# Low parts of the attention probabilities: GpSimd works in eight pieces of 416 columns instead of four of 832

## The chip, the core and the metric

The program runs on one core of a Trainium2 chip. A core has five engines that run at the same time and signal each other by semaphores: TensorE (PE, matrix products), VectorE (DVE), ScalarE (ACT), GpSimd (POOL) and SyncE (SP), which here issues DMAs. The metric is the device time of one execution in microseconds. The kernel before takes 2081.41 us in the median of three runs (2080.66 to 2081.58).

## The reference, cut to what matters

Two graph layers work on x (3327 rows of 256 features) and a 0/1 matrix adj (3327 x 3327). The first is a normalised sum over neighbours. The second runs two attention steps, and of each row of the attention matrix only the largest entries that together hold 0.9 of the mass are kept:

```python
logits = (Xa @ W1) @ W2 @ (Xa @ W3).T
# per row: sort, keep the first k with a cumulated softmax below 0.9, and one more
masked = jnp.where(keep, logits, -jnp.inf)
A  = softmax(masked, axis=1)
Xf = Rf @ Xf ; Xb = Rb @ Xb ; Xa = A @ Xa
Z  = Z + (Xf @ U1[s] + Xb @ U2[s] + Xa @ U3[s])
```

All of it is float32. The change touches only the product `A @ Xa` of the first of the two steps (s = 0).

## The kernel before

The rows are cut into 26 tiles of 128 (NT = 26, the last with 127). The columns are padded to NP = 3328, and HALF is 1664. Each step handles one tile of 128 rows of the attention matrix at a time. The engines' programs are written out by hand, one block for each engine, and keep the order of the code; the tiles overlap by semaphores alone. Loops run over pairs of tiles.

In the first step a tile t goes this way:

- TensorE makes the logits (L1081). VectorE copies them out of PSUM and takes the row maximum (L1388 to L1397). ScalarE turns them into exponentials (L812) as soon as the maximum is there, and then estimates a cut in two passes over the row (L829, L833).
- VectorE ranks the row (`rank`). In two halves it writes what lies below the cut into the sieve (L1508, one input being `expo` twice) and takes the eight largest of seven sections (L1515). L1512, a one-column addition, joins the two sums before the sections of the second half; L1517 follows behind them. Then come rounds of L1531 and L1534 over 112 candidates, a running sum over 32 (the scan, L1536), and a few small instructions (L1538 to L1555), of which L1539 reads two arrays.
- L1576 writes the kept values into `window`, in two halves. The first half waits until the low parts of the tile before have left (`lo_turned`). L1708 ends the tile.
- TensorE multiplies in float16, so the kept values are split: ScalarE writes the high part, in two halves (L870, `natural_hi`), and GpSimd the low part, window minus high part (L633, `natural_lo`). SyncE turns each by a transposing DMA (L502 high, L507 low), and TensorE multiplies the high and then the low part by the two parts of Xa (L1114).
- Beside that ScalarE scales the result of the neighbour sums (L857 to L862), after which GpSimd makes its low part (L624). ScalarE issues the load of the next `s_tile`, 832 KB (L908). GpSimd also adds x to a result tile (L638) shortly before its low parts.

GpSimd's order in a tile is: the pieces of L633, L624, L638. SyncE's order is: L502, a load of queries, L507, the flags of VectorE (L491), and the store of a result.

The low part lies in the same memory as the window. `window_home` has HEAD columns in front of the window, and `natural_lo` starts at its column 0. A piece of 832 float32 columns becomes 832 float16 values, so piece c writes 416 float32 columns' worth of memory, behind what has been read. Between pieces GpSimd drains. HEAD is half of a piece.

Of the kernel before, what the change touches and what calls it, by code (L numbers as in the profile page):

```python
# [22 lines left out]
HALF = NP // 2  # L23
# [28 lines left out]
TRIES = 4.0  # L52
KEPT_AT = (10, 20)
LATE_AFTER = (1, 3)
LO_CHUNK = HALF // 2
HEAD = LO_CHUNK // 2
OVER = 1.000001

# [23 lines left out]
def graph_layers(nc, x, adj, w0, b0, w1, w2, w3, u1, u2, u3, gamma, beta, out):  # L82
    ctx = ExitStack()
    with ctx:
# [3 lines left out]
        def sem(name):  # L88
            return ctx.enter_context(nc.semaphore(name))
# [227 lines left out]
        hi_made = sem("hi_made")  # L317
# [246 lines left out]
        def _(pool):  # L564
# [61 lines left out]
            def probs_low(t):  # L626
                for c in range(NP // LO_CHUNK):
                    cols = slice(c * LO_CHUNK, (c + 1) * LO_CHUNK)
                    if c > 0:
                        pool.drain()  # L630
                    if c % 2 == 0:
                        pool.wait_ge(hi_made, t * 2 + c // 2 + 1)
                    last = G.tensor_tensor(natural_lo[:, cols], window[:, cols], natural_hi[:, cols], ALU.subtract)  # L633
                last.then_inc(lo_made, 1)

# [4 lines left out]
            def low_parts(t, m, b):  # L640
                probs_low(t)
                if not (isinstance(t, int) and t == 0):
                    diffused_low(t, m, b)
                    add_x(t - 1, m - 1 + b, 1 - b)
# [1139 lines left out]
```

## Time and profile before

| | |
|---|---|
| median of three runs | 2081.41 us (2080.66 to 2081.58) |
| the profiled execution | 2080.55 us, span 2078.9 us |
| busy: TensorE matmul | 1784.7 us (86%) |
| busy: VectorE | 1667.7 us (80%) |
| busy: ScalarE | 1365.0 us (66%) |
| busy: GpSimd | 555.4 us (27%) |
| L633, 104 instructions | 223.0 us busy, mean 2144 ns |
| L1508, its largest form, 56 instructions | 150.6 us busy, mean 2689 ns |
| L507 and L502, 26 each | median landing 4.9 and 5.8 us after issue |

The span is the time from the first to the last instruction of the profiled execution. Shares of busy time are averages over stages with different limits. The first attention step lies between about 360 and 1105 us, the second behind it. Rows of the timeline give start and duration in us, the engine, the line of the program, the operation, what it writes and reads, the shapes, a count if several were merged, and in brackets the idle time before and what ended it. "SPq" and "ACTq" are instructions of a queue, such as the issue of a DMA.

### The profile page before, as it was taken

Reading aid. Unit: us, or ns where it says so; the run is one execution under the profiler, and the core shown is the slowest. Engines: PE = TensorE matmul, PEld = TensorE weight load, DVE = VectorE, ACT = ScalarE, POOL = GpSimd, SP = SyncE. Lnnn points to the kernel's source line nnn. Section 1 sums busy time; section 2 is a strip of 40 time slices with the busy share of each in tenths; the row PEclk is TensorE's granted clock in tenths of the full one; section 3 lists DMA queues with packets and bytes.
Section 4 is the critical chain, followed back from the end, with each engine's and each line's share of the span. In section 5 each row is a group of like instructions: output and inputs, shape, how many; then the busy total and the mean of one; then the engine's idle time right before and its main releaser. Section 6 shows DMA issues by size and latency. Waiting matters only on the chain.

```text
span 2078.9 us, 37636 instructions
## 1 busy us (share of the span) xinstructions
PE 1784.7 (86%) x11660; PEld 1314.5 (63%) x11660; DVE 1667.7 (80%) x4213; ACT 1365.0 (66%) x2157; POOL 555.4 (27%) x869
## 2 busy tenths in 40 slices
PE   3999953899999999994765299999999999999997
PEld 2888831677777777773653166666666666666665
DVE  6444465899999999998851699999989999999996
ACT  5222266788888888884622586867676767677752
POOL 4000030343333333332230113131313232222220
PEclk9999976899999999997988699999999999999999
DMA  6999621444444444442333001010101010101022
GB/s 156 197 203 207 165 99 39 104 113 112 112 112 112 112 109 106 107 111 55 75 79 112 21 21 41 20 40 20 40 20 40 20 40 22 39 24 37 31 93 69
DMA packets 235346, 168.27 MB, mean 81 GB/s; under 512 B 188451, under 2 KB 220577, under 8 KB 235168
## 3 DMA queue, kind: packets, MB, share of 16 engines
q1 hardware_dynamic: 221264, 117.44, 20.8%
q0 software_dynamic: 3744, 22.14, 6.9%
q10 hardware_dynamic: 10288, 28.12, 4.0%
q8 instruction: 19, 0.31, 0.1%
q14 instruction: 31, 0.25, 0.0%
HBM read 107.99 MB, written 37.49 MB: 70 GB/s over the span
## 4 chain that ended last, share of the span: by engine, by line
DVE 46%; PE 18%; DVEq 17%; issue 11%; ACT 3%; DMA 3%; POOLq 0%; ACTq 0%; POOL 0%; SPq 0%
DVE probs_t L1508 7%; DVE stats L1525 5%; DVE stats L1515 5%; DVE window L1405 4%; DVEq L1706 4%; DVE scraps L1405 4%; DVE sorted_e L1534 2%; DVE window L1568 2%; DMA probs_t<-astray 2%; DVEq L1572 2%; DVE expo L1388 2%; DVEq L1532 2%; PE lg L1081 2%; PE bank L1029 2%; PE bank L1028 2%
## 5 line engine op out<-in xcount | busy, mean ns | idle before, releaser
L1081 PE MATMUL lg<-k_t,q_tile 64*128 64x512 f32 (+1 forms) x832 | 199.5, 582 | 134.3 <-DVE expo L1388 105.6
L1104 PE MATMUL bank<-both,s_tile 128*128 128x512 f16 x1352 | 300.1, 379 | 0.0
L1171 PE MATMUL bank<-xcur,probs_t 128*128 128x256 f32 x1352 | 296.1, 379 | 0.0
L1171 PEld LDWEIGHTS bank<-xcur,probs_t 128*128 128x128 f32 x1352 | 254.9, 190 | 33.6
L633 POOL TENSOR_TENSOR window<-window,probs_t 128x832 f16<-128x832 f32 x104 | 223.0, 2144 | 112.7 <-ACT probs_t L870 100.0
L1388 DVE TENSOR_SCALAR_CACHE_REDUCE expo<-lg 128x1024 f32 (+1 forms) x208 | 205.0, 1022 | 41.3 <-PE lg L1081 30.8
L1104 PEld LDWEIGHTS bank<-both,s_tile 128*128 128x128 bf16 x1352 | 132.3, 98 | 148.1
L1081 PEld LDWEIGHTS lg<-k_t,q_tile 64*128 64x128 f32 x832 | 72.2, 196 | 221.0 <-DVE expo L1388 134.3
L812 ACT ACTIVATE expo<-expo,neg_max 128x3327 f32<-128x3327 f32 x52 | 159.4, 3065 | 73.1 <-DVE neg_max L1397 73.1
L659 POOL TENSOR_TENSOR aims<-found 128x2 f32<-128x2 f32 x26 | 5.1, 194 | 649.0 <-ACT found L838 649.0
L833 ACT ACTIVATE turned<-expo,found 128x3327 uint8<-128x3327 f32 x52 | 159.7, 3071 | 3.6
L829 ACT ACTIVATE turned<-expo,found 128x3327 uint8<-128x3327 f32 x52 | 159.5, 3066 | 2.2 <-issue 0.4
L1104 PE MATMUL bank<-parts,s_tile 128*128 128x256 f16 x1352 | 159.9, 275 | 0.0
L1114 PE MATMUL bank<-parts,turned_lo 128*128 128x256 f16 x1352 | 155.4, 274 | 3.2 <-DMA turned_lo<-window 3.2
L930 ACT ACTIVATE probs_t<-bank 128x512 f32<-128x512 f32 (+1 forms) x182 | 94.9, 564 | 93.6 <-PE bank L1160 92.5
L1508 DVE SCALAR_TENSOR_TENSOR probs_t<-expo,mine 128x1664 f32 (+3 forms) x56 | 150.6, 2689 | 4.7 <-issue 4.1
L1114 PE MATMUL bank<-parts,turned_hi 128*128 128x256 f16 x1352 | 153.8, 272 | 0.0
L1160 PE MATMUL bank<-ident,window 128*128 128x128 f32 x676 | 99.4, 287 | 55.3 <-DVE kept_inv L1708 47.6
L1114 PEld LDWEIGHTS bank<-parts,turned_lo 128*128 128x128 f16 x1352 | 132.5, 98 | 22.3 <-DMA turned_lo<-window 3.8
L1114 PEld LDWEIGHTS bank<-parts,turned_hi 128*128 128x128 f16 x1352 | 131.8, 98 | 22.1 <-DMA turned_hi<-probs_t 1.5
L1104 PEld LDWEIGHTS bank<-parts,s_tile 128*128 128x128 bf16 x1352 | 133.0, 98 | 18.2
L1127 PE MATMUL bank<-u_sb,turned 128*128 128x256 f32 x624 | 143.2, 379 | 0.0
(291 smaller groups left out, 3642.8 us busy)
## 6 DMA issues: line engine op xcount, KB each, us to landing
s_tile<-s_scratch SPq DMA_DIRECT2D x28, 832.0 KB, 4.5
expo<-in_adj POOLq DMA_DIRECT2D x25, 831.8 KB, 9.8
s_tile<-s_scratch ACTq DMA_DIRECT2D x24, 832.0 KB, 4.4
s_scratch<-s_tile SPq DMA_DIRECT2D x14, 832.0 KB, 9.8
s_scratch<-probs_t SPq DMA_DIRECT2D x6, 832.0 KB, 9.8
s_scratch<-window SPq DMA_DIRECT2D x6, 832.0 KB, 10.5
q_tile<-q_scratch SPq DMA_DIRECT2D x104, 32.0 KB, 2.1
xa_scratch<-ht ACTq DMA_DIRECT2D x26, 128.0 KB, 1.9
```

The costliest lines, as they stand in the source:

```text
L633: last = G.tensor_tensor(natural_lo[:, cols], window[:, cols], natural_hi[:, cols], ALU.subtract)
L812: A.activation(expo[b][:, 0:N], expo[b][:, 0:N], ACT.Exp, bias=neg_max[b], accum_out=total[b])
L829: A.activation(seen, sample, ACT.Sign, scale=-1.0, bias=tried[b][r], accum_out=signs[:, :])
L833: A.activation(seen, sample, ACT.Relu, scale=-1.0, bias=tried[b][r], accum_out=lack[:, :])
L1081: last = T.matmul(lg[c % 2][:, h * CHUNK:h * CHUNK + w], q_tile[b][DA * h:DA * (h + 1), :], k_all[DA * h:DA * (h + 1), s, c0:c0 + w], star ...
L1104: last = T.matmul(s_ps[:, 0:width], s_tile[b][:, k, :], moving, start=(k == 0 and part == 0), stop=(k == NT - 1 and part == 1))
L1114: last = T.matmul(kept_ps[0][:, 0:D], turned_p[:, k, :], parts[:, k, part * D:(part + 1) * D], start=(p == 0 and k == 0 and part == 0), st ...
L1127: last = T.matmul(pv_ps[:, 0:D], turned_part[:, c, :], u_sb[:, j, c, :], start=(not begun and j == 0 and c == 0), stop=(j == 2 and c == DC ...
L1171: last = T.matmul(kept_ps[1][:, 0:D], probs_t[:, k * P:(k + 1) * P], xcur[:, k, :], start=(k == 0), stop=(k == NT - 1))
L1388: V.tensor_scalar(exps_of_halves(b, c0, c0 + w), lg[c % 2][:, :].rearrange("p (h n) -> p h n", h=2)[:, :, 0:w], 1.0, None, ALU.mult, ALU.m ...
L1405: V.scalar_tensor_tensor(out=out, in0=exps(b, 0, N), scalar=cut, in1=exps(b, 0, N), op0=ALU.is_lt, op1=ALU.mult, accum_out=under[:, :])
L1508: V.scalar_tensor_tensor(out=sieve[:, 0:c1 - c0], in0=exps(b, c0, c1), scalar=cut, in1=exps(b, c0, c1), op0=ALU.is_lt, op1=ALU.mult, accum ...
```

## The change

The width of a piece of the low parts, LO_CHUNK, is a quarter of HALF instead of a half: 416 columns instead of 832. A tile's low parts are eight instructions instead of four, each but the first behind a drain. GpSimd still waits twice for ScalarE's high parts, once before the first piece and once before the first piece of the second half; the two conditions are written so that they follow LO_CHUNK. HEAD, which is LO_CHUNK // 2, is 208 columns instead of 416, so `window_home` is 208 columns shorter.

```diff
@@ -52,7 +52,7 @@
 LATE_AFTER = (1, 3)
-LO_CHUNK = HALF // 2
+LO_CHUNK = HALF // 4
 HEAD = LO_CHUNK // 2
@@ -628,8 +628,8 @@
                     if c > 0:
                         pool.drain()
-                    if c % 2 == 0:
-                        pool.wait_ge(hi_made, t * 2 + c // 2 + 1)
+                    if c * LO_CHUNK % HALF == 0:
+                        pool.wait_ge(hi_made, t * 2 + c * LO_CHUNK // HALF + 1)
                     last = G.tensor_tensor(natural_lo[:, cols], window[:, cols], natural_hi[:, cols], ALU.subtract)
                 last.then_inc(lo_made, 1)
```

GpSimd's instructions from the end of the stage before to the first tiles of the step. L618 belongs to the stage before, L382 is the loop over pairs of tiles, and a row with "window<-window,probs_t" is a piece of the low parts (the low part lies in the window's memory, the high part in that of probs_t):

```order
 L618 TENSOR_TENSOR parts<-xcur,parts 128x256 x26
 L624 TENSOR_TENSOR both<-xfb,both 128x512
-L633 TENSOR_TENSOR window<-window,probs_t 128x832 x4
+L633 TENSOR_TENSOR window<-window,probs_t 128x416 x8
 L382 UNCONDITIONAL_BRANCH
 L382 ISA
-L633 TENSOR_TENSOR window<-window,probs_t 128x832 x2
+L633 TENSOR_TENSOR window<-window,probs_t 128x416 x4
 L632 REGISTER_ALU
-L633 TENSOR_TENSOR window<-window,probs_t 128x832 x2
+L633 TENSOR_TENSOR window<-window,probs_t 128x416 x4
 L623 REGISTER_ALU
 L624 ISA
```

Each row of 832 columns has become two of 416 in the same place. Nothing else on GpSimd moves, and the instructions of the other four engines are the same in number and order.

## Rows read from the trace of the kernel before

**Rows 1.** The page: share of the span by engine in the chain that ended last.

```profile
DVE 46%; PE 18%; DVEq 17%; issue 11%; ACT 3%; DMA 3%; POOLq 0%; ACTq 0%; POOL 0%; SPq 0%
```

**Rows 2.** ScalarE in order of time (start us, us, instruction): two neighbouring tiles.

```profile
654.69 3.07 ACT L870 ACTIVATE probs_t<-window 128x1664 f16<-128x1664 f32 x2 [0.23 <-issue]
...
658.65 3.07 ACT L812 ACTIVATE expo<-expo,neg_max 128x3327 f32<-128x3327 f32 x1 [0.53 <-DVE neg_max L1397]
...
680.89 3.06 ACT L870 ACTIVATE probs_t<-window 128x1664 f16<-128x1664 f32 x2
...
685.17 3.07 ACT L812 ACTIVATE expo<-expo,neg_max 128x3327 f32<-128x3327 f32 x1 [0.86 <-DVE neg_max L1397]
```

**Rows 3.** ScalarE in order of time: the first L870 ten tiles later.

```profile
918.59 3.07 ACT L870 ACTIVATE probs_t<-window 128x1664 f16<-128x1664 f32 x2 [0.23 <-issue]
```

**Rows 4.** GpSimd in order of time, one tile of the first step.

```profile
654.64 0.72 POOL L638 TENSOR_TENSOR y_tile<-y_tile,xcur 128x256 f32<-128x256 f32 x1 [8.35 <-ACT y_tile L889]
...
656.36 3.69 POOL L633 TENSOR_TENSOR window<-window,probs_t 128x832 f16<-128x832 f32 x2 [0.99 <-ACT probs_t L870]
...
660.25 5.08 POOL L633 TENSOR_TENSOR window<-window,probs_t 128x832 f16<-128x832 f32 x2 [0.20 <-issue]
...
671.48 1.16 POOL L624 TENSOR_TENSOR both<-xfb,both 128x512 f32 x1 [6.16 <-ACT both L862]
```

**Rows 5.** All instructions of L633: least, median and greatest duration in ns.

```profile
L633 POOL TENSOR_TENSOR window<-window,probs_t x104: 1757/1770/3236, 364.8 to 1082.6; 128x832 f16<-128x832 f32 x104
```

**Rows 6.** VectorE in order of time, the same tile.

```profile
658.58 3.21 DVE L1508 SCALAR_TENSOR_TENSOR probs_t<-expo,mine 128x1664 f32 x1
...
664.30 2.77 DVE L1508 SCALAR_TENSOR_TENSOR probs_t<-expo,mine 128x1663 f32 x1 [0.17 <-issue]
...
667.15 0.16 DVE L1512 TENSOR_TENSOR under<-sieved 128x1 f32<-128x1 f32 x1
...
672.26 0.46 DVE L1536 TENSOR_TENSOR_SCAN prefix<-sorted_e,prefix 128x32 f32<-128x32 f32 x1
...
674.31 1.95 DVE L1576 SCALAR_TENSOR_TENSOR window<-expo,below 128x1663 f32 x1
...
678.94 0.16 DVE L1708 RECIPROCAL kept_inv<-cells 128x1 f32 x1 [0.18 <-issue]
```

**Rows 7.** VectorE in order of time: L1508 and the scan with GpSimd idle.

```profile
354.67 0.29 DVE L1536 TENSOR_TENSOR_SCAN prefix<-sorted_e,prefix 128x32 f32<-128x32 f32 x1
...
945.00 1.95 DVE L1508 SCALAR_TENSOR_TENSOR probs_t<-expo,mine 128x1664 f32 x1
```

**Rows 8.** VectorE and GpSimd in order of time, near the end of the step.

```profile
1053.75 9.85 POOL L633 TENSOR_TENSOR window<-window,probs_t 128x832 f16<-128x832 f32 x4 [28.70 <-ACT probs_t L870]
...
1057.20 2.87 DVE L1508 SCALAR_TENSOR_TENSOR probs_t<-expo,mine 128x1663 f32<-128x1663 f32 x1
...
1060.15 1.56 DVE L1512 TENSOR_TENSOR under<-sieved 128x1 f32<-128x1 f32 x1
```

**Rows 9.** DMA issues in order of time, the same tile as Rows 6.

```profile
665.35 3.35 SPq L507 DMA_TRANSPOSE turned_lo<-window  x1
...
670.74 0.35 ACTq L908 DMA_DIRECT2D s_tile<-s_scratch  x1
```

**Rows 10.** The tile turned_lo: all 26 of its loads, issue to landing.

```profile
DMA to landing us min/median/max: 4.8/4.9/8.7
```

**Rows 11.** SyncE, ScalarE and VectorE in order of time: the load that took longest.

```profile
1011.42 4.06 SPq L507 DMA_TRANSPOSE turned_lo<-window  x1
...
1014.19 0.35 ACTq L908 DMA_DIRECT2D s_tile<-s_scratch  x1
...
1020.15 1.95 DVE L1576 SCALAR_TENSOR_TENSOR window<-expo,below 128x1663 f32<-128x1663 f32 x1 [1.48 <-DMA turned_lo<-window]
```

**Rows 12.** TensorE in order of time, the same tile as Rows 6.

```profile
673.22 5.91 PE L1114 MATMUL bank<-parts,turned_lo 128*128 128x256 f16 x52
...
680.38 1.64 PE L1081 MATMUL lg<-k_t,q_tile 64*128 64x512 f32 x8 [1.25 <-DVE expo L1388]
```
## The prediction

> **What bounds the kernel now.** I read the chain of waits first. The reader is to see that VectorE carries it [rows 1]. In order of time the chain shows that in the first attention step (about 360 to 1105 us) it runs through VectorE's row work on a tile, with L1508 as its largest line. Then the timeline of one tile, engine by engine. The step has 26 tiles; L870 starts at 654.69 and ten tiles later at 918.59, so a tile takes 26.39 us [rows 2, 3]. The even pattern starts eight tiles before the first of these and ends with the last, 19 tiles in all. The others are the three at the start and four at the end.
>
> ScalarE waits 0.53 and 0.86 us for VectorE before L812 [rows 2], and TensorE 1.25 us before its late logits [rows 12]. So both would follow a faster VectorE a little, and VectorE sets the pace. GpSimd is not the bound, but it meets VectorE. L633 takes 1.77 us in the median and 3.24 at most [rows 5]: in the tile shown the first two are 1.77 each with 0.15 between (3.69), and the second pair is 3.17 + 0.14 + 1.77 (5.08) [rows 4]. L1508 takes 1.95 us with GpSimd idle [rows 7], but here 3.21 and 2.77 [rows 6].
>
> The times fit one rule to 0.02 us: an L1508 and an L633 exclude each other for their whole length. The second L633 holds from 658.27 to 660.05. L1508 starts at 658.58, waits, and ends at 661.79, which is 1.74 after 660.05 (1.95 less about 0.21 of start-up). The third L633 started at 660.25, waits for 661.79 and ends at 663.42, 1.63 later (1.77 less 0.14). The second L1508 starts at 664.30, the fourth L633 ends at 665.33, and 1.74 later is its end, 667.07.
>
> The same lock holds small VectorE instructions with two inputs in SBUF. L1512 takes 0.16 us when GpSimd has finished [rows 6] but 1.56 at 1060.15, where the third L633 had been waiting behind L1508 [rows 8]. The Trainium skill, SBUF — State Buffer, "Who interferes with whom", says that a VectorE instruction with two SBUF inputs and a GpSimd one that reads SBUF exclude each other, and names no least size. By that rule L1512 loses its turn below; were it free, the tile would go as in the first rival.
>
> One more collision decides. L624 is started by ScalarE, 12.83 us after L812, and runs from 671.48 to 672.64 [rows 2, 4]. The scan L1536 takes 0.29 us alone [rows 7]. Here it starts at 672.26, ends at 672.72 [rows 6], 0.08 after L624, and L1576 follows 1.59 later. The arrival at the scan is therefore not what sets L1576: anything that comes between 671.6 and 672.4 leaves at 672.72.
>
> **The change part by part.** It splits every L633 in two: 104 instructions of 832 columns go, 208 of 416 come, with a drain before each. ScalarE's halves, the waits on them and the DMAs are as many as before.
>
> The length of a piece. The trace has 256 columns in 0.72 us, 512 in 1.16 [rows 4] and 832 in 1.77 [rows 5]. The line through the last two gives 0.98 for 416, that through the first two 0.995. I take 0.98, with 0.84 after a wait. The ends are half of 1.77, 0.885 (a piece costs nothing of its own), and 1.16 (that of 512 columns). The Trainium skill, GPSIMD Engine Reference, "Elementwise — side-by-side cycle accounting", gives about 2.6 cycles an element at 1.2 GHz, an estimate of 0.90 us for 416 columns before any cost of issue; by it the sum would come out near the first rival.
>
> GpSimd alone: 8 x 0.98 + 6 x 0.14 + 0.20 = 8.88 us for 4 x 1.77 + 2 x 0.14 + 0.20 = 7.56, so 1.3 more. Behind it on its engine stand L624 and the next tile's L638, both with us to spare; SyncE's load of turned_lo (L507) and with it TensorE's low products and VectorE's L1576 wait for its end.
>
> Now the tile of the rows, by the lock, with the new pieces. P1 656.36 to 657.34, P2 to 658.46, P3 from 658.60 to 659.58. L1508 asks at 658.79, behind P3, and ends at 659.58 + 1.74 = 661.32 (was 661.79, gain 0.47). P4, held up, ends at 662.16, P5 at 663.34, P6 at 664.46. The second L1508 starts 2.51 after the first's end, at 663.83, and ends at 664.46 + 1.74 = 666.20 (was 667.07, gain 0.87 now). P7, waiting, takes the lock and ends at 667.04. L1512 should run at 666.28; it waits to 667.12, where before it ended at 667.31. So 0.68 of the 0.87 is given back and 0.19 is left. The scan comes at 672.07, still inside L624, and leaves at 672.72 as before. The gain is swallowed: 0 a tile. Nor does the start of L1508 shift against the pieces, since L1576 and all behind it keep their times.
>
> P8 ends at 668.16, so L507 starts 2.8 us later than 665.35 [rows 9]. Usually it lands 4.9 us after its issue [rows 10]: 673.06 instead of 670.25. TensorE wants it at 673.22 and could lose 1.25 more [rows 12]; VectorE wants it at 674.31 [rows 6]. That cover is 1.25 us thick. Its price when gone comes from a loop over two tiles: L870 to first piece 1.67, pieces 11.80, landing 4.9, L1576 to the end of L1708 4.79, to the next L812 6.07, to the next L870 22.24 [rows 2, 4, 6]. The sum is 51.47 for two tiles, against 2 x 26.39 = 52.78; before it was 48.64. So it binds once a landing takes more than 6.2 us.
>
> The uneven tiles. At the start the same working gives VectorE shorter waits before the scan, and later landings for which nobody waits: 0, between -0.5 and +1. At 1020.15 L1576 already waits for turned_lo [rows 11]. There the pieces, from 1000.98, would end at 1012.82 instead of 1011.40: +1.4, or -0.8 if the slow landing does not come back. In the tile at 1053.75 [rows 8] the pieces end at 65.0 instead of 63.6, a landing of 4.9 gives 1069.9, and L1576, at 1069.16 now, waits: +0.8. In the last tile VectorE is done and 1.3 us later is hidden under TensorE's high products. Sum of the edges: +2.2, between -1.3 and +3.5. At 1.16 a piece the scan still arrives in time, at 672.35, but the last piece ends at 669.6 and L1576 waits 0.2: 19 x 0.2 = +4 beside the edges. At 0.885 a piece comes the first rival.
>
> HEAD is half of LO_CHUNK, so the window array starts 832 bytes nearer to its home, and every later array moves by as much. No row prices this; I take 0, since all durations above are in columns, and up to 1 us either way.
>
> The sum: the profiled execution took 2080.55 us (span 2078.9 and 1.65 around it), 0.86 below the median of 2081.41. 2080.55 + 0 + 2.2 = 2082.75; by the median 2083.6. I say 2083.0.
>
> **Rivals.** First, faster: the shorter waits get through. With pieces of 0.885 the first L1508 ends at 661.04, the second at 665.64, L1512 at 666.47, and the scan comes at 671.42, just ahead of L624. It passes; then L1539, also of two inputs, waits for 672.64, and L1576 starts 1.1 after it, 0.5 sooner than now. 19 x 0.5 is 10 us: 2073 with the edges. For it: L1508 loses 1.26 + 0.82 us a tile today, and shorter pieces do shorten that. Against: the scan has to be 0.6 us earlier than I find, and both lines through the rows say 0.98. ScalarE, which has 0.53 to give in every other tile, caps it. Chance 0.17.
>
> Second, slower: the low load gates VectorE. It now starts 2.6 us ahead of the big load of s_tile (L908 at 670.74) instead of 5.4 [rows 9]. In the one tile with 2.77 between them it took 8.7 us [rows 10, 11]. With 8.7 everywhere the loop over two tiles is 55.27, so 27.64 a tile: +1.25 x 19 = 24 us, 2107. It decides from a landing of 6.2 us on. Against: there the issue itself took 4.06 instead of 3.35 us, so that load was slow by itself before the other was issued at 1014.19, and the overlap that I expect is under 1 us at the tail. Chance 0.10.
>
> Third, slower by a little: the pieces cost more than 0.98 (up to 1.16), or a small two-input instruction behind L1512 loses another turn. Then L1576 goes 0.2 to 0.5 late a tile: 4 to 10 us, 2087 to 2092. Chance 0.17.
>
> **How the numbers follow.** The forecast has 0.56; its own range is 2079 to 2086. A measurement of this kernel tells about 0.2%, 4.2 us, from no change: 2077.2 to 2085.6. Of the forecast nearly all lies inside, 0.53, with 0.03 above. The first rival is faster in nearly all (0.17, and 0.01 from elsewhere). The other two are slower, 0.25 of their 0.27. So faster 0.18, same 0.54, slower 0.28. The range of 8 in 10 takes in most of the first and third: 2071 to 2092.
>
> **What would show it.** Right: L633 with a median of about 0.98 us and 2.4 where held up; the first L1508 at about 2.7 and the second at 2.4 instead of 3.21 and 2.77; L1512 at 0.8 instead of 0.16; the scan longer than its 0.46; L870 to L870 still 26.39; L507 2.8 us later against L812. Wrong: a scan of 0.29 with an earlier L1576 (first rival), L1576 put down to turned_lo in every tile (second), pieces of 1.1 us and more (third). The number is wrong if the period of a tile moves by 0.2 us or more.

## The result, and the profile after

The changed kernel takes 2107.38 us in the median of four runs (2104.83 to 2109.14), the kernel before 2081.36 in the same comparison. The ratio is 1.0125, 95% interval 1.0107 to 1.0142: slower by 1.25%. The forecast was 2083 with 2071 to 2092; the time that came is that of the second rival, 2107, to which I had given 0.10.

The page of the changed kernel: its span, the chain that ended last by engine and by line, and two groups of instructions (busy us, mean ns, idle time before and what ended it).

```profile
span 2104.2 us, 37844 instructions
...
DVE 28%; PE 24%; ACT 12%; issue 11%; DVEq 11%; POOLq 6%; DMA 5%; ACTq 2%; POOL 1%; SPq 0%
POOLq L630 6%; PE bank L1114 5%; DVE stats L1525 5%; DMA turned_lo<-window 4%; DVE window L1405 4%; DVE scraps L1405 4%; DVEq L1706 3%; ACT scraps L829 3%; ACT scraps L833 3%; PE lg L1081 3%; DVE window L1568 2%; DVEq L1572 2%; ACT expo L812 2%; PE bank L1029 2%; PE bank L1028 2%
...
L633 POOL TENSOR_TENSOR window<-window,probs_t 128x416 f16<-128x416 f32 x208 | 262.9, 1264 | 129.9 <-ACT probs_t L870 102.2
...
L1114 PE MATMUL bank<-parts,turned_lo 128*128 128x256 f16 x1352 | 175.5, 295 | 43.9 <-DMA turned_lo<-window 43.8
```

VectorE's share of the chain has fallen from 46% [rows 1] to 28, and three things stand there that were not among its large lines before: GpSimd's queue at the low parts (6%), the load of turned_lo (4%), and the products that wait for it (L1114, 5%). In the stretch from 600 to 680 us they are over half of the chain: the load 20.7%, L1114 20.0%, GpSimd's queue 12.4%. What waits for that load, and how long the load takes, least, median and most:

```profile
  PEld bank L1114: 47.6, 13
  PE bank L1114: 43.8, 12
  DVE window L1576: 33.3, 13
...
DMA to landing us min/median/max: 4.8/5.1/8.8
```

Thirteen of the 26 tiles wait, L1576 2.6 us each on average. Twelve of them have a landing of 7.8 us or more. In order of time, two neighbouring tiles; first ScalarE with its issue of the s_tile load, to be held against [rows 2, 9]:

```profile
654.01 0.35 ACTq L908 DMA_DIRECT2D s_tile<-s_scratch  x1
...
664.79 3.07 ACT L870 ACTIVATE probs_t<-window 128x1664 f16<-128x1664 f32 x2 [0.72 <-DVE kept_inv L1708]
671.20 3.07 ACT L812 ACTIVATE expo<-expo,neg_max 128x3327 f32<-128x3327 f32 x1 [2.98 <-DVE neg_max L1397]
...
683.31 0.35 ACTq L908 DMA_DIRECT2D s_tile<-s_scratch  x1
...
693.45 3.06 ACT L870 ACTIVATE probs_t<-window 128x1664 f16<-128x1664 f32 x2
697.08 3.07 ACT L812 ACTIVATE expo<-expo,neg_max 128x3327 f32<-128x3327 f32 x1 [0.20 <-DVE neg_max L1397]
```

SyncE's issues of the low load:

```profile
652.17 3.32 SPq L507 DMA_TRANSPOSE turned_lo<-window  x1
...
676.81 3.32 SPq L507 DMA_TRANSPOSE turned_lo<-window  x1
```

VectorE, which answers to [rows 6]:

```profile
660.00 1.95 DVE L1576 SCALAR_TENSOR_TENSOR window<-expo,below 128x1663 f32 x1 [2.34 <-DMA turned_lo<-window]
...
676.22 2.31 DVE L1508 SCALAR_TENSOR_TENSOR probs_t<-expo,mine 128x1663 f32 x1 [0.17 <-issue]
...
686.51 1.94 DVE L1576 SCALAR_TENSOR_TENSOR window<-expo,below 128x1663 f32 x1
...
703.93 0.77 DVE L1512 TENSOR_TENSOR under<-sieved 128x1 f32<-128x1 f32 x1
```

The two tiles differ. The load issued at 652.17 has L908 1.84 us behind it and lands at 659.97, after 7.8 us. VectorE waits, and L812 comes 6.41 us after L870 instead of 3.96, and with it L908, which ScalarE reaches some 12 us after L812. So the next low load, at 676.81, has L908 6.50 us behind it and lands in 4.9. VectorE catches up, L812 is only 3.63 us behind L870, and the tile after has the collision again. One tile takes 26.12 us and the next 28.66. From tile 3 (L870 at 444.00) to tile 21 (941.19) the mean is 27.62 us, against 26.38 over the same tiles before. The 18 tiles take 497.2 us instead of 474.8: 22.4 of the 25.3 by which the span grew.

### The profile page after: what moved, and what is told of

Same layout as the page of the kernel before. It is cut to its first block, busy times and chain, and to the rows that moved or that the text cites. A ratio compares the mean times of both kernels' runs of the same rounds, so it can differ in the third digit from the quotient of the medians.

```text
span 2104.2 us, 37844 instructions
## 1 busy us (share of the span) xinstructions
PE 1800.8 (86%) x11660; PEld 1323.3 (63%) x11660; DVE 1656.1 (79%) x4213; ACT 1365.3 (65%) x2157; POOL 597.4 (28%) x973
## 4 chain that ended last, share of the span: by engine, by line
DVE 28%; PE 24%; ACT 12%; issue 11%; DVEq 11%; POOLq 6%; DMA 5%; ACTq 2%; POOL 1%; SPq 0%
POOLq L630 6%; PE bank L1114 5%; DVE stats L1525 5%; DMA turned_lo<-window 4%; DVE window L1405 4%; DVE scraps L1405 4%; DVEq L1706 3%; ACT scraps L829 3%; ACT scraps L833 3%; PE lg L1081 3%; DVE window L1568 2%; DVEq L1572 2%; ACT expo L812 2%; PE bank L1029 2%; PE bank L1028 2%
## 5 line engine op out<-in xcount | busy, mean ns | idle before, releaser
L633 POOL TENSOR_TENSOR window<-window,probs_t 128x416 f16<-128x416 f32 x208 | 262.9, 1264 | 129.9 <-ACT probs_t L870 102.2
L812 ACT ACTIVATE expo<-expo,neg_max 128x3327 f32<-128x3327 f32 x52 | 159.4, 3066 | 89.0 <-DVE neg_max L1397 89.0
L1114 PE MATMUL bank<-parts,turned_lo 128*128 128x256 f16 x1352 | 175.5, 295 | 43.9 <-DMA turned_lo<-window 43.8
L1114 PEld LDWEIGHTS bank<-parts,turned_lo 128*128 128x128 f16 x1352 | 141.8, 106 | 75.6 <-DMA turned_lo<-window 47.6
L1114 PE MATMUL bank<-parts,turned_hi 128*128 128x256 f16 x1352 | 154.0, 273 | 0.3 <-DMA turned_hi<-probs_t 0.3
L1114 PEld LDWEIGHTS bank<-parts,turned_hi 128*128 128x128 f16 x1352 | 132.0, 98 | 22.5 <-DMA turned_hi<-probs_t 1.8
L1160 PEld LDWEIGHTS bank<-ident,window 128*128 128x128 f32 x676 | 74.3, 144 | 105.3 <-DVE kept_inv L1708 68.0
```

Source lines behind the costliest of these rows:

```text
L812: A.activation(expo[b][:, 0:N], expo[b][:, 0:N], ACT.Exp, bias=neg_max[b], accum_out=total[b])
L1114: last = T.matmul(kept_ps[0][:, 0:D], turned_p[:, k, :], parts[:, k, part * D:(part + 1) * D], start=(p == 0 and k == 0 and part == 0), st ...
L1160: last = T.transpose(flip_ps[g % 2][:, k * P:(k + 1) * P], window[:, (k0 + k) * P:(k0 + k + 1) * P], ident[:, :])
```

## The experiments

All of them in one table. The landing is that of turned_lo in the even stretch, "behind" the distance from L507 to L908 there.

| kernel | median, us | ratio to before, 95% | a tile, us | L908 behind | landing |
|---|---|---|---|---|---|
| changed | 2107.38 | 1.0125 [1.0107, 1.0142] | 27.62 | 1.8-2.2 / 4.5-7.7 | 7.8-8.8 / 4.8-5.1 |
| e1 changed, load late | 2074.12 | 0.9965 [0.9953, 0.9978] | 26.20 | 11 | 4.9 |
| e2 before, low load 2.6 or 4.1 us later | 2154.95 | 1.0345 [1.0328, 1.0362] | 29.69 | 0.6 / 5.5 | 9.9-10.5 / 4.9 |
| e3 changed, a quarter of the load | 2079.03 | 0.9993 [0.9983, 1.0002] | 26.39 | 2.6-2.9 | 5.7-5.8 |
| e4 changed, HEAD 416 | 2108.08 | 1.0132 [1.0115, 1.0149] | 27.67 | 1.8-2.1 / 4.5-7.7 | 7.8-8.9 / 4.9 |
| e5 before, load late | 2082.60 | 1.0008 [0.9999, 1.0016] | 26.48 | 12-14 | 4.9 |
| e6 half of the change | 2086.95 | 1.0057 [1.0031, 1.0083] | 26.45 | 3.3-3.5 | 4.9 |
| e7 e1, L624 after L638 | 2073.01 | 0.9962 [0.9949, 0.9974] | 26.05 | 10.4-11 | 4.9 |
| e8 changed, load early | 2077.15 | 0.9984 [0.9974, 0.9993] | 26.32 | ahead, by 4.3-4.6 | 4.9 |
| e9 e7 with 2 x 832, 4 x 416 | 2072.70 | 0.9964 [0.9950, 0.9978] | 26.04 | 11.1-11.6 | 4.9 |

**e1, the load of s_tile issued late.** In ScalarE's `first_step`:

```diff
-                    if more:
-                        act.wait_ge(s_done[0], t + 3)
-                        act.dma_start(flat(s_tile[b][:, :, :]), ...)
                     if before is not None:
                         query_key(*before)
                     if more:
                         refine(b, 1)
+                        act.wait_ge(s_done[0], t + 3)
+                        act.dma_start(flat(s_tile[b][:, :, :]), ...)
```

> The changed kernel with eight pieces, where ScalarE issues the load of s_tile (L908) some 9 us later, after its second estimate, so that it starts after the low load has landed. Theory A (the low load lands late because the load of s_tile is issued 1.8 to 2.2 us behind it): turned_lo lands 4.9 us after issue in every tile, L1576 never waits for it, a tile takes 26.4 us and the time is 2079 to 2085. Theory B (the low load is slow by itself, or VectorE and GpSimd lose the time at their lock): still 2100 or more.

Landings are 4.8 to 4.9 in the even stretch, and the time is not only back: it is 7.5 us below the kernel before, better than I had written, and a tile takes 26.20 us instead of 26.4. L1576 waits for the low load in two tiles only, both outside the even stretch. Theory B falls.

**e2, the old pieces, the end of the low parts delayed.** In `probs_low`, LO_CHUNK as before:

```diff
                     last = G.tensor_tensor(natural_lo[:, cols], window[:, cols], natural_hi[:, cols], ALU.subtract)
+                for _ in range(12):
+                    pool.drain()
+                    last = G.memset(aims[:, :], 0.0)
                 last.then_inc(lo_made, 1)
```

> The kernel before, with four pieces of 832 columns, and behind the last piece 12 memsets of two columns with a drain before each, about 2.8 us in which GpSimd reads nothing. The low load then starts as late as with eight pieces, but VectorE meets the old pieces. Theory A (late issue, then collision with the load of s_tile): turned_lo lands after 7.8 us or more where L908 is issued less than 2.8 us behind it, tiles alternate between long and short, and the time is 2095 to 2110. Theory B (the shorter pieces themselves cost the time at the lock): no more than 2085.

The theory holds in kind and misses in size: 2155. With the old pieces the waits at the lock put the low load further back in every other tile (14.8 us after L870, where eight pieces give 13.5), L908 is only 0.56 us behind, and the landing takes 10 us. Here the issue itself is drawn out as well, to 7.9 to 8.5 us in these tiles:

```profile
672.36 8.00 SPq L507 DMA_TRANSPOSE turned_lo<-window  x1
```

So a later low load is enough for a loss, with no short piece in the kernel. That the short pieces made the loss smaller (13.5 instead of 14.8 us) is not shown, since the two runs differ in the distance between the loads too.

**e3, a quarter of the bytes.** L908 loads `[:, 0:NP // 4]` of the tile, as said in the expectation.

> The changed kernel, which loads only the first quarter of each s_tile in the first step (208 instead of 832 KB); the neighbour sums are computed from the rest of an older tile. The issue stays where it is. Theory A1 (the collision costs the bytes that overtake the low load): a landing falls from 8 us to about 5.7, under the 6.2 that the loop allows, and the time to 2080 to 2088. Theory A2 (it is the issue of a second load in the middle of the first that costs, whatever its size): landings stay at 7.8 and the time at 2100 or more.

A1 holds: 5.7 or 5.8 us, as written, in every tile from 2 to 21, with L908 1.9 to 2.9 us behind (from tile 4 on 2.6 to 2.9). The bytes of the second load matter, and not only that it is issued. VectorE in one tile of it:

```profile
658.06 2.74 DVE L1508 SCALAR_TENSOR_TENSOR probs_t<-expo,mine 128x1664 f32 x1
...
663.30 2.37 DVE L1508 SCALAR_TENSOR_TENSOR probs_t<-expo,mine 128x1663 f32 x1 [0.17 <-issue]
...
665.75 0.77 DVE L1512 TENSOR_TENSOR under<-sieved 128x1 f32<-128x1 f32 x1
671.47 0.73 DVE L1536 TENSOR_TENSOR_SCAN prefix<-sorted_e,prefix 128x32 f32<-128x32 f32 x1
673.79 1.95 DVE L1576 SCALAR_TENSOR_TENSOR window<-expo,below 128x1663 f32 x1
```

This is the tile of the forecast. I had 2.74 for the first L1508, 2.37 for the second, L1512 ending 0.68 late (0.77 is 0.61 more than its 0.16), and the scan still inside L624. The tile takes 26.39 us, as before.

**e4, the addresses.** `HEAD = LO_CHUNK` instead of `LO_CHUNK // 2`.

> The changed kernel with HEAD left at 416 columns, so that window and all later arrays stand at their old addresses. Theory A (the addresses play no part): as the changed kernel, 2104 to 2110, with the same alternation of landings. The rival, that the shift of the addresses makes the transposing load slow: 2083.

As the changed kernel, 2108.08 with the same alternation. The shifted addresses play no part in the loss.

**e5, the control for e1.** The same edit in the kernel before.

> The kernel before, pieces of 832 columns, with only the load of s_tile issued late as in the first experiment. A control for it. Theory A (with pieces of 832 there was no collision to remove, and the gain of the first experiment comes from the shorter pieces): 2079 to 2083, a tile takes 26.39 us, the scan still waits for L624. Rival (the late load is worth 7 us by itself): 2074.

The late load gains nothing with the old pieces: the ratio is 1.0008, with 1 inside its interval. The gain of e1 (0.9965) needs the eight pieces too. In two details this run is not as written: a tile takes 26.48 us, and the scan waits for L624 only in every other tile (0.43 to 0.48 us, 0.28 or 0.29 in the others).

**e6, two pieces of 832 and four of 416.** The loop runs over `[HALF // 2] * 2 + [HALF // 4] * 4`, HEAD is 416.

> Half of the change: the first half of a row in two pieces of 832, the second in four of 416, HEAD as before. The load of s_tile is where it was. By the lock the last piece ends some 0.7 us earlier than with eight, so L908 comes about 3.3 us behind the low load. Theory A with an edge (from 3.15 us on a load landed in 4.8): all landings 4.9, 26.4 us a tile, 2080 to 2083. Theory A without an edge, the landing growing as the distance shrinks: landings between 5 and 7.8, 2081 to 2095.

The landing has an edge in these rows (none lies between 5.1 and 7.3 us), but the kernel stands on it. In the profiled execution tiles 5 to 21 are even, with L908 3.3 to 3.9 us behind and landings of 4.8 to 5.0; three tiles elsewhere had 2.51, 2.84 and 2.11 us and took 7.6, 7.3 and 9.2. The nine runs fall into two groups, five at 2083.4 to 2087.0 and four at 2100.5 to 2102.0, so the median of 2086.95 stands for neither. The profiled one is of the first group (2083.54). That the four have more such tiles is likely and was not seen.

**e7, L624 out of the scan's way.** On top of e1, in `low_parts`:

```diff
                 if not (isinstance(t, int) and t == 0):
-                    diffused_low(t, m, b)
                     add_x(t - 1, m - 1 + b, 1 - b)
+                    diffused_low(t, m, b)
```

> The first experiment (eight pieces, late load of s_tile), and GpSimd makes L624 after L638, so that it meets VectorE's start of the next tile and not the scan. Theory S (the scan's wait for L624 is what swallows the shorter waits at L1508): the scan takes 0.29 us in every tile, a tile takes 25.7 to 26.0 us instead of 26.2, and the time is 2066 to 2072. Rival (ScalarE's own 25.7 us and the later first piece, 0.3 to 0.6 us, take the gain back): 2073 to 2078.

Half of theory S holds. The scan takes 0.28 or 0.29 us in every tile of the even stretch, and a tile 26.05 us instead of 26.20. But the time, 2073.0, is the rival's: L812 starts 3.31 to 3.34 us after L870 in all tiles of the even stretch, with no wait before it, so ScalarE no longer waits for VectorE, and from 600 to 680 us the chain that ended last runs through ScalarE. And VectorE has found something else to wait for:

```profile
  DVE window L1575: 20.9, 22
...
DMA to landing us min/median/max: 4.8/4.9/6.6
```

(L1575 is L1576 here.) That is 0.95 us on average in 22 tiles (in the even stretch 0.2 to 0.3 and 1.3 to 1.4 in turn), with the usual landing of 4.8 to 5.0.

**e8, the load of s_tile early.** The edit of e1 the other way: the two lines stand before `refine(b, 0)`.

> The changed kernel with the load of s_tile issued early instead of late: before ScalarE's first estimate, some 6 us sooner, so that it has moved before the low load starts. Theory A (only a load of s_tile issued within 3 us behind the low load delays it; one that is ahead does no harm): turned_lo lands after 4.9 us in the even tiles, about 26.2 us a tile, 2072 to 2078. Rival (any big load near the transposing ones delays one of them, here the high one, or ScalarE waits for TensorE before the issue): landings of turned_hi over 6.5 us or a longer ScalarE chain, 2085 and more.

It holds for the distance that was tried, at 2077: a load of s_tile that is 4.3 to 4.6 us ahead does no harm, and turned_hi lands after 5.8 us in the median as everywhere. Nearer than that is open: in tile 1 it was 2.41 us ahead and the low load took 7.0, but the same tile takes 6.4 and 6.6 in e1 and e7. The tile is that of the forecast again (scan 0.98 and 0.73, 26.32 us), while e1 runs in another phase (below).

**e9, both and the mixed pieces.**

> The late load, L624 after L638, and two pieces of 832 in the first half with four of 416 in the second, so that the low parts end 0.7 us earlier. Before, with eight pieces, L1576 waited for turned_lo in every tile. If that wait is what is left: 25.9 us a tile and 2068 to 2072. If ScalarE is (its L812 waited for nothing in 2073): 26.0 and 2071 to 2074.

The second: ScalarE is the bound. The wait of L1576 has shrunk to 0.2 to 0.3 us, and the time has not moved; L812 again follows 3.33 us after L870, a tile takes 26.04 us, and the chain from 600 to 680 us is ScalarE's. By their intervals e1, e7 and e9 are not told apart, and e1 is the smallest edit.

## Why the prediction was wrong

**Pieces and lock: right.** L633 has a median of 0.976 us (0.98 taken). From L870 to the low load are 13.47 to 13.50 us in nearly all tiles of the even stretch in e1, e3 and e8, where I had 1.67 + 11.80 = 13.47. In the changed kernel that is so in every other tile; the others, in which VectorE comes late, have 12.0 in the main. L1508, L1512 and the scan came as worked out, shown in e3 at the forecast's own phase. Least, median and most of them in the changed kernel, in ns:

```profile
L633 POOL TENSOR_TENSOR window<-window,probs_t x208: 969/976/2713, 363.1 to 1110.7; 128x416 f16<-128x416 f32 x104
```

```profile
L1512 DVE TENSOR_TENSOR under<-sieved x27: 159/766/774, 374.1 to 1085.1; 128x1 f32<-128x1 f32 x27
```

**The step that failed** is the one sentence "Usually it lands 4.9 us after its issue: 673.06 instead of 670.25". I moved the load by 2.8 us and kept its duration. Moved, it had L908 2.6 us behind it by my own times, and every low load in this study with the full load of s_tile less than 3 us behind it took 7.3 us or more (every such load is in the table but those of e4, which repeats the changed kernel with 7.8 to 8.9):

| L908 behind L507 | landing | where |
|---|---|---|
| 0.18 us | 9.5 | e2, tile 23 |
| 0.5-0.6 | 9.9-10.5 | e2, ten tiles |
| 1.8-2.2 | 7.8-8.8 | changed, twelve tiles |
| 2.11 | 9.2 | e6, tile 23 |
| 2.51 | 7.6 | e6 |
| 2.77 | 7.8 | e2, tile 0 |
| 2.77 | 8.7 | before, tile 23 [rows 11] |
| 2.84 | 7.3 | e6 |
| 3.15 | 4.8 | before, tile 2 |
| 3.26 and more | 4.8-5.1 | all kernels, even stretches |

The trace before holds both ends: the 8.7 us with 2.77 between [rows 11], and tile 2, with 3.15 between, which landed in 4.8:

```profile
430.08 3.29 SPq L507 DMA_TRANSPOSE turned_lo<-window  x1
...
433.23 0.35 ACTq L908 DMA_DIRECT2D s_tile<-s_scratch  x1
```

I took the 8.7 for a load that was slow by itself before the other was issued, since its issue took 4.06 us instead of 3.35. The times don't say that: an issue of 3.35 from 1011.42 would have ended at 1014.77, and L908 came at 1014.19. And it was a part of it only. With no load of s_tile near it, the same tile takes 5.8 us (e7), 5.9 (e1), 6.1 (e5, again with an issue of 4.06), 6.5 (e8, where it is 5.1 us ahead) and 7.0 (e9). So 0.9 to 2.1 us are its own, from a cause that was not looked for, and by e5, the nearest kernel, some 2.6 are the collision.

I had asked only by how much the two loads overlap in time (under 1 us, at the tail). The runs show that the distance and the bytes of the second load decide: 2.4 to 3.9 us more for the full load 1.8 to 2.8 us behind (4.3 in one tile 23), 5.0 to 5.6 at 0.5 to 0.6, and 0.8 for a quarter of it (5.7 less 4.9). One reading fits all rows: a second load issued while L507 is still being issued (3.2 to 3.4 us) gets in front of what is left of it. No run varied that length by itself (in e2 it grew together with the collision), so this reading is not shown.

**The price came out, in part by luck.** The loop over two tiles gave 27.64 us a tile for landings of 8.7, and the kernel has 27.62. That the landings are slow in every other tile only is no difference, since the loop has one landing in two tiles. But its terms were off and made up for each other. Over the eight pairs of tiles from tile 4 to tile 20 the slow landings are 8.16 us on average, 0.54 less than 8.7; L1576 to the end of L1708 is 4.66 instead of 4.79; and from the end of L1708 to L812 are 6.71 instead of 6.07. I had kept the last term fixed. It grows because TensorE gets the low products late and then works at a lower clock (last section), so that VectorE waits for the late logits, in the pair shown with:

```profile
668.88 1.23 DVE L1388 TENSOR_SCALAR_CACHE_REDUCE expo<-lg 128x1024 f32 x1 [0.83 <-PE lg L1081]
```

So in the collision the chain runs from the low load over TensorE's products, and not over L1576 as in my loop. That pair takes 54.76 us: 13.48 to the low load, 7.8 for it, 4.69 to the end of L1708, 6.54 to L812 and 22.25 to the next L870.

**"The gain is swallowed: 0 a tile": right at one phase only.** It is so in e3 and e8. In e1 every other tile gets through. VectorE there, one tile of each sort (L1507, L1535, L1575 are the old L1508, L1536, L1576):

```profile
656.05 2.65 DVE L1507 SCALAR_TENSOR_TENSOR probs_t<-expo,mine 128x1664 f32 x1
...
669.37 1.21 DVE L1535 TENSOR_TENSOR_SCAN prefix<-sorted_e,prefix 128x32 f32<-128x32 f32 x1
...
672.17 1.94 DVE L1575 SCALAR_TENSOR_TENSOR window<-expo,below 128x1663 f32 x1
...
682.65 1.99 DVE L1507 SCALAR_TENSOR_TENSOR probs_t<-expo,mine 128x1664 f32 x1
...
695.32 0.29 DVE L1535 TENSOR_TENSOR_SCAN prefix<-sorted_e,prefix 128x32 f32<-128x32 f32 x1
...
697.93 1.95 DVE L1575 SCALAR_TENSOR_TENSOR window<-expo,below 128x1663 f32 x1
```

In the second the first L1508 slips between two pieces (1.99), the scan comes ahead of L624, and L1576 follows the start of the first L1508 by 15.28 us instead of 16.12. This is the first rival's mechanism, in every other tile and without shorter pieces than I took. So both rivals were in the change at once, the one hiding the other: with the collision 2107, without it 2074 to 2079, and which of these depends on where the load goes. Why the loop settles into one phase or the other was not tried.

**The edges** were worth 2.2 us by my sum. In the changed kernel they can't be read apart from the collision. In e3, which has the forecast's tile, the whole comes out at 2079.0: not told apart from the kernel before (its interval holds 1), and 4 us below the forecast. By my own sum the tile with the slow load (6.3 us there instead of 8.7) gives 2.2 of these 4; the rest is open.

## What to carry to other kernels

When a step makes a DMA start later, list what other engines issue in the window that it moves into, and look in the trace for a transfer that already had such a neighbour; its landing, not the usual one, is the estimate. A cover of 1.25 us on the wait is no cover if the move takes the transfer across an edge of its own duration, here between 2.84 and 3.15 us. And a slowdown may hide a gain: moving one issue turned +1.25% into -0.35%, so the cause is worth a run before a change is dropped.

## What the runs showed of the hardware

Two loads that moved in the same microseconds did not share the time evenly. The later one, of the same 832 KB, issued from ScalarE 1.84 us after SyncE's transposing load, pushed the end of that from 4.9 to 7.8 us. The DMA engines in that stretch, one row a us (stretch, length, granted clock, DMA share, GB/s): 290 GB/s is the transposing load, from 656 on the other one moves beside it.

```profile
653.00:654.00 1.00, 1.00 0.72 166
654.00:655.00 1.00, 1.00 1.27 290
655.00:656.00 1.00, 1.00 1.24 284
656.00:657.00 1.00, 1.00 1.12 325
657.00:658.00 1.00, 1.00 1.03 393
658.00:659.00 1.00, 1.00 0.67 240
659.00:660.00 1.00, 1.00 0.03 7
660.00:661.00 1.00, 0.95 0.00 0
661.00:662.00 1.00, 0.50 0.00 0
```

The Trainium skill, DMA: Bandwidth & Descriptors, "Queues, rings and completion order", says that each DMA engine takes turns between its queues packet by packet. The trace agrees that both move in the same microseconds, but even shares would not give this landing. In the next tile the transposing load moves alone, and lands 0.7 us after the last of these rows' bytes:

```profile
678.00:679.00 1.00, 1.00 1.17 270
679.00:680.00 1.00, 1.00 1.27 290
680.00:681.00 1.00, 1.00 1.26 285
681.00:682.00 1.00, 1.00 0.04 7
```

That is 852 KB. In the collision 740 KB had moved by 656.00, which by the rates leaves an estimated 112 KB of the older load. With even shares of the bytes these would be through before 657, and soon after 658 even if every byte of the row from 655 had been the other load's. A landing would follow some 0.7 us later. The load landed at 659.97, after all 1705 KB of both had moved. No run here shows the turns themselves, nor how large a packet of either load is.

With 0.55 us between the issues (e2) both were slow: the 1705 KB took from 673 to 682, 190 GB/s on average, where the transposing load alone moves 285 to 290, and the other one alone 333 to 353 (685 to 687 in the changed kernel).

The last two rows of the first block show the price on TensorE. It stood idle for 2.96 us before the low products at 660.02, and the granted clock then fell to 0.50, the lower of its two levels (1.2 GHz). The 52 products took 7.57 us instead of 5.91 [rows 12]:

```profile
660.02 7.57 PE L1114 MATMUL bank<-parts,turned_lo 128*128 128x256 f16 x52 [2.96 <-DMA turned_lo<-window]
```

A one-column addition with two inputs (L1512) can lose as much at the lock as a long instruction: it took 0.77 us where it met a piece of 416 and 1.56 where it met one of 832, instead of 0.16. L1508, with 1664 and 1663 columns, lost 0.79 and 0.42 in the tile of e3. What is left of the other engine's instruction sets the wait, not the length of its own.
